# A hand-ordered decoder kernel: state-space taps built from half-wise rate products and moved between partitions by TensorE

## The reference, cut to what matters

```python
s = (q @ k.T) / sqrt(32)                 # 4 heads, 154 context rows per batch
p = softmax over the 32 largest of each row
attended = mean over heads of p @ context
film_in, film_out = attended @ W_film ...     # scales and shifts for 128 channels
u = modulated, normalised x
K = 2 Re( sum_n dC[d,n] * exp(dtA[d,n] * l) ) for lags l = 0..511      # the taps
y = irfft(rfft(u) * rfft(K)) + u * D_skip
y = ffn(layernorm(film_out(y))) ...
```

## Time and profile before

| what | value |
|---|---|
| median of 3 runs | 663.51 us (663.18 to 663.99) |
| the profiled execution, own time | 663.11 us |
| its span | 661.3 us |
| TensorE busy | 603.2 us (91%) |
| VectorE busy | 439.0 us (66%) |
| ScalarE busy | 287.9 us (44%) |
| GpSimd busy | 246.5 us (37%) |

### The profile page before, as it was taken

One profiled execution on the slowest core, in us unless ns is written; L12 is line 12 of the kernel. 1 busy time (PEld: TensorE's weight loads), 2 busy tenths in 40 slices (PEclk: granted clock), 3 DMA queues, 4 the chain that ended last, 5 costly groups with the idle time before them and its releaser, 6 DMA issues.

```text
span 661.3 us, 8811 instructions
## 1 busy us (share of the span) xinstructions
PE 603.2 (91%) x3171; PEld 302.0 (46%) x3172; DVE 439.0 (66%) x1173; ACT 287.9 (44%) x548; POOL 246.5 (37%) x179
## 2 busy tenths in 40 slices
PE   8864959998997999999999998999977999999997
PEld 4432548886572332222222442233622345556566
DVE  6899998556559846766776569668645675333335
ACT  7979968213230554444444333534232334221210
POOL 2899271422531344655465344557334100000001
PEclk9955879999999899999999999999979999999999
DMA  8300006021000000000000000000600000000001
GB/s 321 110 0 0 2 1 256 1 68 60 1 0 1 0 0 1 0 1 1 0 1 0 1 1 0 1 0 1 268 22 1 0 1 0 1 1 0 1 0 33
DMA packets 4945, 19.25 MB, mean 29 GB/s; under 512 B 2053, under 2 KB 3462, under 8 KB 4390
## 3 DMA queue, kind: packets, MB, share of 16 engines
q1 hardware_dynamic: 4902, 18.69, 7.5%
HBM read 18.16 MB, written 0.52 MB: 28 GB/s over the span
## 4 chain that ended last, share of the span: by engine, by line
PE 71%; DVE 14%; ACT 7%; POOL 4%; issue 4%; DMA 0%; POOLq 0%; DVEq 0%; ACTq 0%
PE PS L2401 11%; PE PS L1606 9%; PE PS L1622 8%; PE PS L2422 6%; PE PS L1564 5%; PE PS L1590 3%; PE PS L1692 2%; PE PS L1636 2%; PE PS L1609 2%; DVE SB L1853 2%; DVE SB L199 2%; PE PS L2091 2%; POOL SB L238 2%; ACT SB L468 1%; DVE SB L212 1%
## 5 line engine op out<-in xcount | busy, mean ns | idle before, releaser
L1853 DVE TENSOR_REDUCE SB<-PS 128x2 f32<-128x1024 f32 x64 | 78.4, 1226 | 62.9 <-PE PS L1590 62.8
L1839 POOL TENSOR_TENSOR SB<-SB 128x1024 f32<-128x1024 f32 x32 | 75.2, 2352 | 108.7 <-ACT SB L1791 107.8
L1791 ACT ACTIVATE SB<-PS 128x1024 f32<-128x1024 f32 x64 | 65.6, 1024 | 102.3 <-PE PS L1609 102.2
L2401 PE MATMUL PS<-SB 128*128 128x512 f32 x176 | 78.4, 594 | 0.0
L1606 PE MATMUL PS<-SB 64*128 64x512 f32 x256 | 70.4, 627 | 1.1 <-ACT SB L1795 1.1
L1622 PE MATMUL PS<-SB 128*64 128x512 f32 x256 | 67.6, 610 | 0.5 <-DVE SB L1885 0.5
L238 POOL TENSOR_TENSOR SB<-SB 128x4 f32<-128x4 f32 x18 | 19.3, 1073 | 116.9 <-DVE SB L204 104.3
L2460 ACT ACTIVATE SB<-PS 128x512 f32<-128x512 f32 x44 | 26.2, 597 | 80.2 <-PE PS L2401 78.8
L2486 DVE TENSOR_TENSOR SB<-SB,PS 128x512 f32<-128x512 f32 x44 | 30.0, 688 | 41.8 <-PE PS L2401 40.5
L1876 DVE RECIPROCAL SB<-PS 128x256 f32<-128x256 f32 x32 | 55.6, 1744 | 0.0
L2401 PEld LDWEIGHTS PS<-SB 128*128 128x128 f32 x176 | 32.2, 190 | 35.3 <-issue 33.7
(11 more groups left out here) (415 smaller groups left out, 1125.2 us busy)
## 6 DMA issues: line engine op xcount, KB each, us to landing
SB<-exp SPq DMA_DIRECT2D x1, 4352.0 KB, 14.1
SB<-moe SPq DMA_DIRECT2D x1, 4096.0 KB, 14.5
SB<-dft SPq DMA_DIRECT2D x1, 2304.0 KB, 11.6
SB<-att SPq DMA_DIRECT2D x1, 2048.0 KB, 8.2
SB<-mix SPq DMA_DIRECT2D x1, 768.5 KB, 4.4
SB<-mix SPq DMA_DIRECT2D x1, 640.0 KB, 5.5
SB<-ssm SPq DMA_DIRECT2D x1, 602.0 KB, 6.6
SB<-lat SPq DMA_DIRECT2D x1, 585.0 KB
```

Source lines behind the costliest of these rows:

```text
L1791: act.activation(expd[i % 2][:, 1024 * u:1024 * u + 1024], bank(2 * (u % 2), 2), ACT.Exp).then_inc(sem("d_exp"), 1)
L1839: pool.tensor_tensor(half_sums[half], e[:, 0:1024], e[:, 1024:], ALU.add).then_inc(sem("d_half_sum"), 1)
L1853: dve.tensor_reduce(shift[i % 2][:, qt:qt + DK + 1:DK], two_heads(bank(4, 2)), AX_X, ALU.max, negate=True)\
L2401: pe.matmul(bank(2 * (i % 3) + side), w, xsT[:, 512 * n:512 * n + 512], start=True, stop=True).then_inc(sem(("top2_w1", "top2_w3")[side]), 1)
```

## The change

It has four parts. (a) The low rates signal after each half of the lags, and the low product is split by lag halves instead of channel halves. (b) The taps are copied once as they stand in PSUM into a scratch area, moved between partition groups by 16 TensorE matmuls with 32-column blocks of the identity, and copied once more. The layout of the channels in the taps changes from (g, j) to (j, g), with the loop over channels and the reads adapted. (c) The lists are put in another order: on TensorE `spectrum(2)` ahead of the taps, `spectrum(4)` and `spectrum(5)` earlier; on ScalarE `exponentials(5)` and `scores_in(4)` ahead of the sines; on GpSimd the low products and `modulate` interleaved. (d) The absolute value of the high wave is a helper of its own, a little earlier.

```diff
     def b_pool_high_factor(pool, follow, k):
...
-            pool.wait_ge(sem("s_rates"), 2)
+            pool.wait_ge(sem("s_rates"), 3)
...
     def b_pool_low_factor(pool, h):
-        c = slice(2048 * h, 2048 * h + 2048)
-        pool.wait_ge(sem("s_rates"), 1)
-        pool.wait_ge(sem("s_low_waves"), h + 1)
-        pool.tensor_tensor(low_k[:, c], low_k[:, c], low_e[:, c], ALU.mult).then_inc(sem("s_low_products"), 1)
+        lags = slice(LOW // 2 * h, LOW // 2 * h + LOW // 2)
+        pool.wait_ge(sem("s_rates"), h + 1)
+        pool.wait_ge(sem("s_low_waves"), 2)
+        k, e = lag(low_k, LOW)[:, :, lags], lag(low_e, LOW)[:, :, lags]
+        pool.tensor_tensor(k, k, e, ALU.mult).then_inc(sem("s_low_products"), 1)
...
             ins = act.activation(lag(low_e, LOW)[:, :, l], rate_T, ACT.Exp, scale=float(l))
-        if z == LOW:
-            ins.then_inc(sem("s_rates"), 1)
+        ins.then_inc(sem("s_rates"), 1)
...
-    def b_act_taps(act, a, z):
+    staged = SB[:, W.end:W.end + 512]
+    taps_of = taps.rearrange("p (j c g) -> p c j g", j=4, c=4)
+
+    def b_act_taps(act):
 
         act.wait_ge(sem("s_taps"), 1)
-        tp = bank(3).rearrange("p (g c q) -> p c g q", c=4, q=4)
-        to = taps.rearrange("p (c g j) -> p c g j", c=4, j=4)
-        for q in range(a, z):
-            for j in range(4):
-                act.activation(to[32 * q:32 * q + 32, :, :, j], tp[32 * j:32 * j + 32, :, :, q], ACT.Copy)\
-                   .then_inc(sem("s_taps_copied"), 1)
+        act.activation(staged, bank(3), ACT.Copy).then_inc(sem("s_taps_copied"), 1)
+
+    def b_pe_taps(pe):
+
+        pe.wait_ge(sem("s_taps_copied"), 1)
+        pe.wait_ge(sem("x_scores_in"), NT)
+        block = staged.rearrange("p (g c q) -> p q c g", c=4, q=4)
+        for j in range(4):
+            for q in range(4):
+                ins = pe.matmul(bank(0)[32 * q:32 * q + 32, 128 * j:128 * j + 128], ident[:, 32 * j:32 * j + 32], block[:, q],
+                                start=True, stop=True, tile_position=(0, 32 * q))
+        ins.then_inc(sem("s_taps"), 1)
+
+    def b_act_taps_moved(act):
+
+        act.wait_ge(sem("s_taps"), 2)
+        act.activation(taps, bank(0), ACT.Copy).then_inc(sem("s_taps_copied"), 1)
...
-            for d in range(D):
-                j, g = d % 4, d // 4
+            for d in (32 * j + g for g in range(32) for j in range(4)):
+                j, g = divmod(d, 32)
...
-                pe.wait_ge(sem("s_taps_copied"), 16)
+                pe.wait_ge(sem("s_taps_copied"), 2)
...
-                                    taps[:, 128 * c:128 * c + 128], start=(c == 0), stop=(c == 3))
+                                    taps_of[:, c], start=(c == 0), stop=(c == 3))
...
         gather(4)
+        spectrum(2)
         taps_of_lags()
-        spectrum(2)
         gather(5)
+        b_pe_taps(pe)
         spectrum(3)
         film_tile(4)
         taps_spectrum(0)
         gather(6)
+        spectrum(4)
         film_tile(5)
         taps_spectrum(1)
         film_tile(6)
         gather(7)
-        spectrum(4)
+        spectrum(5)
         film_tile(7)
-        for t in (5, 6, 7):
+        for t in (6, 7):
             spectrum(t)
...
         exponentials(4)
+        b_act_high_sizes(act)
+        exponentials(5)
+        scores_in(4)
         b_act_high_waves(act)
         b_act_low_waves(act)
         b_act_rest_inputs(act)
         attn_in(act, 0)
-        exponentials(5)
         exponentials(6)
         diagonals(1)
         exponentials(7)
-        scores_in(4)
         film_in(0)
...
         diagonals(5)
-        b_act_taps(act, 0, 4)
+        b_act_taps(act)
         exponentials(14)
         attn_in(act, 5)
-        diagonals(6)
+        b_act_taps_moved(act)
         exponentials(15)
         film_in(4)
+        diagonals(6)
         b_act_taps_out(act, 0)
...
         modulate(0)
+        b_pool_low_factor(pool, 0)
         modulate(1)
-        b_pool_low_factor(pool, 0)
         b_pool_low_factor(pool, 1)
+        modulate(2)
         b_pool_high_factor(pool, follow, 3)
-        modulate(2)
         modulate(3)
-        pool.wait_ge(sem("s_taps_copied"), 16)
-        pool.tensor_tensor(taps[0:1, 0:128], taps[0:1, 0:128], skip_line, ALU.add).then_inc(sem("s_taps_in"), 1)
+        pool.wait_ge(sem("s_taps_copied"), 2)
+        first = taps_of[0:1, 0]
+        pool.tensor_tensor(first, first, skip_line.rearrange("p (j g) -> p j g", j=4), ALU.add).then_inc(sem("s_taps_in"), 1)
```

More of the change, by code:

```diff
@@ L542, in b_act_high_rates, with b_act_high_sizes, b_act_high_waves @@
         ins.then_inc(sem("s_rates"), 1)
-    def b_act_high_waves(act):
+    def b_act_high_sizes(act):
         act.wait_ge(sem("s_high_turns"), 2)
         act.activation(high_r, high_t, ACT.Abs).then_inc(sem("s_high_waves"), 1)
+    def b_act_high_waves(act):
         act.wait_ge(sem("s_high_waves"), 1)
```

## The result

The changed kernel takes 659.91 us (median of 20 executions) against 663.87 us for the kernel before (20 executions): 3.96 us less, a ratio of 0.994 with a 95% interval of 0.9927 to 0.9952.

The account below looks back on a forecast made before the run. Three GpSimd operations behind one wait decide when the taps start, with TensorE idle. TensorE's list -4.45, clock +1.0, ScalarE -0.46 give -3.9 us: 659.6 us, range 657.7 to 662.2.

Parts of the forecast that it names:

- Half-wise products (a): GpSimd's low products: the first starts at 70.2, so the taps may start at 90.2 instead of 93.6, 3.4 us sooner.
- ScalarE's order: ScalarE until `film_in(2)`: total work unchanged, a wait gone, so TensorE's and GpSimd's chain comes 0.46 us sooner.
- The early clock: TensorE before `gather(2)`: full clock at 66.5 instead of near 70, removing ScalarE's 0.46 us wait.
- TensorE's order (c): TensorE before the taps: `spectrum(2)` fills 88.4 to 90.4, so the idle 5.2 us is gone.
- The tap stream: The taps matmuls on TensorE: 5.1 us with their gap.
- The clock at the taps: TensorE's clock around the taps: 3.0 us at 0.64, so 1.0 us lost.
- The moves: 16 TensorE matmuls moving the taps: cost 1.7 us, or 2.6 at 1.2 GHz.
- rival 3: Between `gather(5)` and `spectrum(3)`: moves run one after another at 1.2 GHz, 8.2 us instead of 1.7; 666.1; chance 0.07.
- Part (b): Moving the taps: 6.67 us of ScalarE copies removed, two 0.62 us copies and 1.7 us of TensorE matmuls added.
- rival 4: GpSimd's low products: strided access costs twice, so no change, 663.9 us; chance 0.06.

Follow-up runs that it names:

- e2: Changed kernel with the low products split by channels again, both waiting for all 32 low rates; 665.98 us.
- e4: Changed kernel with only `spectrum(2)` put behind the taps again on TensorE; 664.61 us.
- the cut streams: Changed kernel with the taps stream cut after 80 matmuls and `spectrum(3)` put into the cut; 662.21 and 660.38 us without further edits.
- e3: Changed kernel with the old taps layout and sixteen ScalarE copies back, no TensorE moves; 661.41 us.
- e12: Changed kernel with `exponentials(5)` behind the sines, the taps stream cut by `spectrum(3)`, and `film_in(2)` ahead of the high rates; 662.18 us.
- e8: Changed kernel with `exponentials(5)` behind the sines and the taps stream cut by `spectrum(3)`; 661.88 us.
- e10: Second run of the changed kernel with `exponentials(5)` behind the sines and the taps stream cut by `spectrum(3)`; 661.57 us.

## Why the prediction was right

The total was forecast at 659.6 and came out at 659.91, a gain of 3.9 against 3.96. The mechanism held: the taps no longer wait for two products behind one late input, and TensorE's idle stretch is filled. The steps behind the sum did less well than the sum.

- *Half-wise products (a)*: right in kind. Forecast start of the taps 90.2, measured 91.39. e2 shows that this part is what everything rests on: without it the kernel is slower than before.
- *ScalarE's order*: the step that failed. I wrote "Total work on ScalarE until `film_in(2)` is unchanged" and expected it 0.46 us sooner. The work was the same, but the moved `exponentials(5)` had a producer that I did not look up: VectorE's maxima for that pair come at 48.1 us. The added wait of 1.02 us, with some of 0.2 us and less, put `film_in(2)` 0.93 us later instead. That is 1.4 us, against 1.3 between the forecast start of the inverse DFT, 125.8, and the measured 127.07; the misses below cancel but for 0.1.
- *The early clock*: forecast to rise at 66.5, it rose at 65.6, and the 0.46 us wait went. Both terms behind the 66.5 were off: `film_tile(0)` started at 60.05 and not 58.6, and the clock rose 5.6 us after that and not 7.9. That they cancel is luck.
- *TensorE's order (c)*: right, idle closed; e4 shows 2.3 us of it.
- *The tap stream*: 5.1 forecast, 4.76 measured, by two changes that I did not see: 1.4 us less busy at the full clock, 1.06 us more gap. They belong together, as TensorE goes on at the same time after the stream's start either way (last section).
- *The clock at the taps*: forecast 1.0 us lost. It fell 0.2 us behind the stream's end, and the next 3.4 us ran at half speed, which is 1.4 to 1.7 us.
- *The moves*: 1.7 us forecast, 1.80 to 2.04 measured, mostly or all at half speed, where I had 2.6; and 1.96 to 2.56 at full speed (e4 and the cut streams), where I had 1.7. The cost does not follow the clock as the row that I took it from does. Side by side, not one after another: rival 3 is out. Part (b) was costed rightly as no gain (e3).
- *Strided products* (rival 4): 4.63 and 4.68 instead of 4.5; out.

So the stage, forecast at -3.9, gave 2.64 in the first profile and 2.6 between the high wave and the inverse DFT. The other 1.3 us of the measured 3.96 lie in no stretch that two profiles show side by side. The kernel before has only one profile, and its executions scatter as much (662.4 to 666.0 in 20). That the gain agreed within 0.1 us is luck: the stage gave two thirds of it.

## What to carry to other kernels

When an instruction is moved up a queue, look up when its latest input is produced, not only how long it takes: a free-looking reordering cost 1 us here because the producer was 1 us later than the new place. Splitting a product along the axis in which its input arrives lets it start early, here for 0.1 us a product, but only if the queue behind it is arranged for it. When TensorE's list gets shorter, look for the engine that it will meet next: here VectorE's selection took back all of e12's 1 us. And judge a stage of microseconds by the stage in the profile: with scatter of 2 us an execution, medians of a dozen can point the other way.

## What was not expected of the hardware

**Short matmuls outrun their instructions, at a fixed place.** TensorE stands still inside the stream and waits for no semaphore. Kernel before, then the changed one:

```profile
93.61 2.85 PE L735 MATMUL PS<-SB 128*32 128x16 f32 x197 [5.17 <-POOL SB L507]
97.65 1.04 PE L735 MATMUL PS<-SB 128*32 128x16 f32 x59 [1.19 <-issue]
```

```profile
91.39 1.69 PE L750 MATMUL PS<-SB 128*32 128x16 f32 x181
95.33 0.82 PE L750 MATMUL PS<-SB 128*32 128x16 f32 x75 [2.25 <-issue]
```

The place is the same in all profiles that show the gap. Counted from the end of `gather(4)` it comes after 197 matmuls: 197 of the stream in the kernel before and in e4, the 16 of `spectrum(2)` and 181 of the stream in the others; and after 16 + 160 + 16 + 4 = 196 where the stream is cut. The time is nearly the same too: TensorE goes on 3.7 to 4.2 us after the stream's first matmul, at 1.2 or 2.4 GHz, cut or not. (e8 and e10 show no gap at all.) DMA of the changed kernel from 91.4 to 95.4 us (packets, MB, share of 16 engines):

```profile
q8 instruction: 1, 0.02, 2.1%
```

In all 14 profiles a packet of 16 KB of this kind starts 1.2 to 1.6 us after the stream, and where there is a gap TensorE goes on 1.3 to 1.6 us after the packet has ended. This queue carries 25 such packets in the changed kernel, for 6,408 matmuls and weight loads. So TensorE very likely waits for the next block of its own list; no run moved the blocks, so this is argued and not shown. The cut does not bring the instructions sooner. It puts 2 us of other work into the time until they come, and 2.25 us of gap become 0.19 to 0.39 or none.

**A race between VectorE and GpSimd ahead of the stage.** VectorE rounds the high angles (L484) just as GpSimd starts its first subtraction (L494). Kernel before, VectorE and then GpSimd:

```profile
29.43 1.23 DVE L484 TENSOR_SCALAR SB<-SB 128x2048 f32<-128x2048 f32 x1 [0.81 <-ACT SB L475]
```

```profile
29.59 5.45 POOL L494 TENSOR_TENSOR SB<-SB 128x2048 f32<-128x2048 f32 x1
```

The changed kernel's third profile, VectorE and GpSimd:

```profile
29.34 4.51 POOL L494 TENSOR_TENSOR SB<-SB 128x2048 f32<-128x2048 f32 x1
29.42 5.51 DVE L484 TENSOR_SCALAR SB<-SB 128x2048 f32<-128x2048 f32 x1 [1.06 <-ACT SB L475]
```

If VectorE is first, by 0.04 to 1.05 us, it takes 1.2 to 2.1 us and GpSimd 5.4 to 5.6 instead of 4.5. If GpSimd is first, by 0.08 us here and 0.02 in e10, VectorE takes 5.5 to 5.6, and everything on ScalarE behind it is 3.6 us later (the high wave starts at 48.9 instead of 45.3). It happened in two of the 14 profiles, in kernels whose lists are the same up to there. The Trainium skill (SBUF — State Buffer, "Who interferes with whom") says that the two engines share a port pair, that a VectorE instruction in a two-port mode, which `tensor_scalar` can enter, contends for it with GpSimd, and that whoever issues first holds it for the whole instruction while the other blocks. The trace agrees: GpSimd's instruction ends at 33.85, and VectorE's ends 1.1 us later, about its own time. Letting GpSimd wait for VectorE's rounding should take this lottery out; it was not tried.
